# A vision tower on one core: GpSimd's sums of absolute differences, one image's set in two parts

## The reference, cut to what matters

```python
def one_query(qs):
    return -jnp.sum(jnp.abs(qs[:, None, :, :] - k), axis=-1) * scale
...
v = (x @ wqv_w.T + wqv_b).reshape(b, t, 3 * h, d)
q, vf, vb = (v[:, :, :h], v[:, :, h:2 * h], v[:, :, 2 * h:])
k = x[:, :, None, :] * wk[None, None]
a = _l1_scores(q, k)
a = jnp.concatenate([a, jnp.zeros((b, 1, t, h), a.dtype)], axis=1)
a = jax.nn.softmax(a, axis=1)[:, :t]
bf = jnp.einsum('bsdh,bshw->bdhw', a, vf)
bb = jnp.einsum('bdsh,bshw->bdhw', a, vb)
o = (bf + bb).sum(axis=2).reshape(b, t, d)
```

## Time and profile before

| | us |
|---|---|
| median of 3 runs | 2366.63 |
| lowest, highest | 2364.35, 2366.93 |
| the profiled execution, its whole time | 2366.79 |
| its span in the profile | 2365.0 |
| VectorE busy | 2054.4 (87%) |
| TensorE busy | 2158.9 (91%) |
| GpSimd busy | 1710.9 (72%) |
| ScalarE busy | 1693.7 (72%) |

### The profile page before, as it was taken

The page is one execution under the profiler, slowest core; times in us unless marked ns, Lnnn a source line. Parts: engine busy times, 40 slices in busy tenths (PEclk is TensorE's granted clock), DMA queues, the critical chain, the costliest instruction groups (busy, mean ns, idle before and its releaser), DMA issues.

```text
span 2365.0 us, 48508 instructions
## 1 busy us (share of the span) xinstructions
PE 2158.9 (91%) x13383; PEld 999.3 (42%) x13383; DVE 2054.4 (87%) x2501; ACT 1693.7 (72%) x4540; POOL 1710.9 (72%) x975
## 2 busy tenths in 40 slices
PE   5475999999888999999999999999999999999978
PEld 4352333333333444444444444444444444444456
DVE  2877777778879999999999999999999999999963
ACT  1232443333458888888888888888888888888865
POOL 0111433333468999999999999999999999999923
PEclk9797999999999999999999999999999999999979
DMA  4301333333312222222222222222222222222201
GB/s 130 84 1 36 77 78 77 77 75 73 73 48 52 52 53 57 57 53 54 53 56 57 55 54 53 55 57 56 53 53 54 57 57 54 53 53 57 57 12 30
DMA packets 169432, 135.54 MB, mean 57 GB/s; under 512 B 45661, under 2 KB 151070, under 8 KB 169247
## 3 DMA queue, kind: packets, MB, share of 16 engines
q1 hardware_dynamic: 159850, 118.02, 20.2%
q10 hardware_dynamic: 9532, 16.91, 3.0%
HBM read 10.51 MB, written 4.19 MB: 6 GB/s over the span
## 4 chain that ended last, share of the span: by engine, by line
DVE 32%; PE 31%; issue 11%; ACT 1%; DVEq 0%; SPq 0%; ACTq 0%; DMA 0%
DVE score L1673 30%; PE pp L943 9%; PE pp L931 4%; PE pp L880 3%; PE pp L849 3%; PE pp L842 2%; PE pp L875 2%; PE pp L1037 1%; PE pp L935 1%; PE pp L890 1%; PE pp L1028 1%; PE pp L734 1%; PE pp L1046 1%; PE pp L1020 0%; DVE absd L1621 0%
## 5 line engine op out<-in xcount | busy, mean ns | idle before, releaser
L1673 DVE TENSOR_REDUCE score<-pp 128x16 f32<-128x1024 f32 x1280 | 1480.0, 1214 | 80.8 <-PE pp L943 80.6
L1805 POOL TENSOR_TENSOR absd<-absd 128x2560 f32<-128x2560 f32 x635 | 1449.1, 2282 | 80.2 <-ACT absd L1252 39.4
L943 PE MATMUL pp<-blocks,pick 128*128 128x512 f16 x2560 | 757.3, 383 | 48.8 <-DVE score L1673 34.3
L1252 ACT ACTIVATE absd<-pp 128x512 f32<-128x512 f32 x1280 | 696.2, 599 | 78.3 <-PE pp L931 59.0
L931 PE MATMUL pp<-blocks,pick 128*128 128x512 f16 x1280 | 394.1, 381 | 1.8 <-ACT absd L1252 1.5
L943 PEld LDWEIGHTS pp<-blocks,pick 128*128 128x128 f16 x2560 | 192.1, 97 | 437.6 <-DVE score L1673 339.3
L1776 POOL TENSOR_TENSOR absd<-absd,yw 128x512 f32<-128x512 f32 x112 | 147.4, 1316 | 293.4 <-DVE yw L1605 293.2
L1196 ACT ACTIVATE absd<-pp 128x512 f32<-128x512 f32 x256 | 149.6, 597 | 205.0 <-PE pp L785 136.2
L1621 DVE SCALAR_TENSOR_TENSOR absd<-pp,absd 128x512 f32<-128x512 f32 x256 | 171.6, 686 | 76.0 <-ACT absd L1196 60.7
L931 PEld LDWEIGHTS pp<-blocks,pick 128*128 128x128 f16 x1280 | 119.0, 97 | 193.2 <-ACT absd L1252 43.3
L1282 ACT ACTIVATE expd<-attn 128x65 f32<-128x65 f32 x512 | 156.5, 315 | 0.0
(11 more groups left out here) (244 smaller groups left out, 2644.0 us busy)
## 6 DMA issues: line engine op xcount, KB each, us to landing
blocks<-qk SPq DMA_DIRECT2D x1032, 64.0 KB, 2.0
blocks<-gT SPq DMA_DIRECT2D x128, 128.0 KB
blocks<-gT ACTq DMA_DIRECT2D x128, 128.0 KB
attn<-score SPq DMA_DIRECT2D x256, 64.0 KB, 2.1
xs<-xn SPq DMA_DIRECT2D x66, 32.0 KB, 1.8
big<-in_wrb_t SPq DMA_DIRECT2D x1, 2064.0 KB
big<-in_x_rows SPq DMA_DIRECT2D x4, 512.0 KB, 6.0
token_rows<-big SPq DMA_DIRECT2D x8, 256.0 KB, 2.0
```

The lines of the kernel that those rows point to most:

```text
L943: mm = pe.matmul(ps[bank + n], pick[:, unit % 8 + n, :], blocks[:, b, unit // 16, unit // 8 % 2, :], start=True, stop=True)
L1252: nc.scalar.activation(absd[odd][:, 16 * u + 8 * n:16 * u + 8 * n + 8, :], ps[4 + n].rearrange("p (h w) -> p h w", w=D), ACT.Abs).then_inc ...
L1673: dve.tensor_reduce(score[:, odd, b, 16 * d:16 * d + 16], pp[:, bank:bank + 2, :].rearrange("p n (h w) -> p (n h) w", w=D), AX.X, ALU.add, ...
L1805: nc.gpsimd.tensor_tensor(x[:, :, 0:w], x[:, :, 0:w], x[:, :, w:2 * w], ALU.add).then_inc(X["tree"], 1)
```

## The change

Before, GpSimd waits for the absolute values of all five A tiles of an image, and sums the 80 rows with five additions and a sixth that writes to `score`. After, it takes the first three tiles (48 rows) when those are there, with five additions and a sixth, and then the other two (32 rows) when those are there, again with five and a sixth. The wait for the DMA that reads `score` stands before the first of the two writes, and "pooled" is counted once, by the second.

```diff
-                x = absd[b]
-                pool.wait_ge(X["abs"], 2 * NA * s + 2 * NP)
-                for m, w in enumerate((32, 16, 8, 4, 2)):
-                    if m:
-                        pool.wait_ge(X["tree"], 5 * s + m)
-                    nc.gpsimd.tensor_tensor(x[:, :, 0:w], x[:, :, 0:w], x[:, :, w:2 * w], ALU.add).then_inc(X["tree"], 1)
-                pool.wait_ge(X["tree"], 5 * s + 5)
-                if at >= 2:
-                    pool.wait_ge(X[f"spread{b}"], SPREAD * (p - 1))
-                nc.gpsimd.tensor_tensor(score[:, odd, b, 16 * ND:16 * ND + 16 * NP].unsqueeze(2), x[:, :, 0:1], x[:, :, 1:2],
-                                        ALU.add).then_inc(X["pooled"], 1)
+                x, n = absd[b], 10 * s
+                for lo, hi in ((0, 3), (3, NP)):
+                    part = x[:, 16 * lo:16 * hi, :]
+                    pool.wait_ge(X["abs"], 2 * NA * s + 2 * hi)
+                    for m, w in enumerate((32, 16, 8, 4, 2)):
+                        if m:
+                            pool.wait_ge(X["tree"], n + m)
+                        nc.gpsimd.tensor_tensor(part[:, :, 0:w], part[:, :, 0:w], part[:, :, w:2 * w], ALU.add).then_inc(X["tree"], 1)
+                    n += 5
+                    pool.wait_ge(X["tree"], n)
+                    if at >= 2 and lo == 0:
+                        pool.wait_ge(X[f"spread{b}"], SPREAD * (p - 1))
+                    op = nc.gpsimd.tensor_tensor(score[:, odd, b, 16 * (ND + lo):16 * (ND + hi)].unsqueeze(2), part[:, :, 0:1], part[:, :, 1:2],
+                                                 ALU.add)
+                op.then_inc(X["pooled"], 1)
```

## The result

The changed kernel takes 2526.55 us in the median of four runs (2525.83 to 2527.29), against 2366.32 (2364.35 to 2366.93) before: 1.0679 times as long, with a 95% interval of 1.066 to 1.0697. The profiled execution has a span of 2524.0 us. The prediction on record was 2520.

A forecast was written before the change was run, and what follows sets the result against it. VectorE with TensorE was taken as the bound, with GpSimd level and becoming the bound at B = 13.61 us a batch. Span 674.5 + 2.7 + 126 B + 125.7 = 2517.8, so 2520 us, 6.5% slower; range 2470 to 2565 us at 0.79.

The forecast's parts named there:

- The bound: Amid the stage VectorE with TensorE sets the period, 12.285 us an image; GpSimd needs 12.14 and has 0.14 to spare.
- The cost of a batch: GpSimd's additions for one image grow from 12.145 by 1.46 to 13.61 us, summed by instruction size.
- The upper end of the range: A batch of 13.97 us, from 0.30 us per added GpSimd instruction, giving 2565 us.
- What the price is: Each added GpSimd instruction costs about 0.25 us whatever its size, not a price per row.
- the rival of cheap instructions: Small GpSimd additions overlap, so a split costs little more than its gaps: 2392 to 2470 us, chance 0.11.
- The page's rule: Documentation's 4497 ns for a 2048-element GpSimd addition leaves 60 ns for the rest: batch 12.96, time 2438 us.
- Where the wait goes: In the stage ScalarE waits for GpSimd's buffers, about 1 us an image, TensorE behind it, VectorE behind TensorE; SyncE costs nothing.
- the 0.88 of the sum: TensorE's clock decides only under a mean of 12.0 / 13.61 = 0.88; that rival had chance 0.01.
- GpSimd never waits: Once behind, GpSimd finds an image's five tiles ready after 10.3 us, while its batch s starts 13.6 after.
- The tail: VectorE's last sum comes 14.1 us after batch 125, then 111.57 us unchanged to the end of the span.
- The rival on the other side: Hidden: buffers' 2.05 us and GpSimd's idle time in the head absorb its lag; time stays 2367 us, chance 0.03.
- the line through the whole stage: Span is 802.9 + 126 B, B being GpSimd's batch time; it reaches 2365.0 at B = 12.40.

The follow-up runs named there:

- The alternating order: Changed kernel's twelve additions and two waits, with the two parts' additions taken in turn, each waiting only for the last but one: 2392.97 us, ratio 1.0107.
- the four-and-one split: Changed kernel with its two parts cut as four tiles and one instead of three and two: 2528.18 us, ratio 1.069 to the kernel before.
- the changed kernel in the loop alone: Changed kernel with two parts only from image 7 on, images 0 to 6 summed whole as before: 2516.93 us, ratio 1.0636.
- one image in four: Changed kernel with two parts only for the second image of every odd pair, the others summed whole: 2400.86 us, ratio 1.0136.
- the seven additions: Kernel before with only the first addition split, into 1536 and 1024 elements, both after the wait for all five tiles: 2369.26 us, ratio 1.0008.
- the alternating loop: Alternating kernel with its order only from image 7 on, images 0 to 6 summed whole with six additions: 2366.88 us, ratio 0.9999 to the kernel before.
- the alternating ones: Twelve additions with the parts taken in turn, throughout (2392.97 us) or only in images 0 to 6 with the loop's sets whole (2390.68 us).

## Why the prediction was right

**The bound.** Right. GpSimd stood 0.14 us an image under the kernel's pace, and took the chain as soon as its batch grew. A kernel whose page has GpSimd at 72% had it at 12.14 of 12.285 us in the stage that counts.

**The cost of a batch.** Forecast 13.61, measured 13.62. By term, start to start: 1536 elements 3.541 forecast and 3.433 + 0.079 = 3.512 measured, 1024 2.461 and 2.429, 768 1.914 and 1.919, 512 1.363 and 1.350; the two writes 0.39 and 0.22 + 0.19 = 0.41. About 0.05 of the mean is a pause of 0.22 us at the turn of the loop, once in four batches, which the sum did not have at all; small errors the other way made up for it. The upper end of the range had a slip: 12.145 + 6 x 0.30 is 13.95, not 13.97.

**What the price is.** Half right. I called 0.25 us what an instruction costs whatever its size. The alternating order shows two parts. About 0.13 us is there only when an instruction needs the one just before: a gap of 0.079 and an overlap of 0.05 forgone. The rest, about 0.14 us, is the instruction's own: the twelve durations sum to 12.9 us, the six to 11.7, which is 0.19 each for six more, less 0.05 of overlap. The batch of six has five such steps, the one before the write with 0.14 instead of 0.08, 0.71 us together; the change adds six instructions and five such steps, 6 x 0.14 + 5 x 0.13 = 1.49 us, and the batch grew by 1.47. Alternation adds the six and takes the first five steps away, 0.84 - 0.71 = 0.13, and with the pause at the turn of the loop 0.18; the pace grew by 0.17 to 0.18, from 12.145 to 12.31 and 12.33. The 0.14 and 0.05 are worked out from means, and not measured one by one. The durations alone grew by 1.08 us, from 11.73 to 12.82, where the rival of cheap instructions had about 0.70. The forecast held because the change runs each part as a chain, like the rows that I read. The cheap rival had the right mechanism, overlap, for a program that was not this one.

**The page's rule.** The Trainium skill, "GPSIMD Engine Reference", section 3.1, has 4497 ns for an addition of 2048 elements. The trace of the four-and-one split has 4510: it agrees. But what I took from the page for the rest of an instruction, 60 ns, does not: 16 elements take 216 ns. The estimate from the page, 2438 us, was 89 us short.

**Where the wait goes.** Right along the whole line of waits, with ScalarE at 71.0 us in 600, or 1.6 us an image, where I had written about 1. TensorE's clock cost nothing, as forecast: it was 0.96 to 0.99 against the 0.88 of the sum. SyncE's queue cost nothing that shows: among the waits from 1200 to 1800 us none is for a DMA.

**GpSimd never waits.** Wrong in the head, right after it. Timeline of GpSimd, first parts of batches 0, 2, 4, 7 and 8:

```profile
672.88 7.52 POOL L1807 TENSOR_TENSOR absd<-absd 128x1536 f32<-128x1536 f32 x5 [12.49 <-ACT absd L1252]
...
700.85 8.37 POOL L1807 TENSOR_TENSOR absd<-absd 128x1536 f32<-128x1536 f32 x5 [1.05 <-ACT absd L1252]
...
731.83 7.46 POOL L1807 TENSOR_TENSOR absd<-absd 128x1536 f32<-128x1536 f32 x5 [2.29 <-ACT absd L1252]
...
776.13 9.20 POOL L1807 TENSOR_TENSOR absd<-absd 128x1536 f32<-128x1536 f32 x5 [2.67 <-ACT absd L1252]
...
791.42 7.51 POOL L1807 TENSOR_TENSOR absd<-absd 128x1536 f32<-128x1536 f32 x5
```

GpSimd waits 19.6 - 12.5 = 7.1 us for ScalarE in all, five times up to batch 7. Batch 8 starts at 791.42; the sum had 674.5 + 2.7 + 8 x 13.61 = 786.1, which is even earlier than the 787.33 of the kernel before. This is most of what the forecast lacked. Of the 6.2 us between spans of 2517.8 and 2524.0, the start was 1.6 us earlier, the eight batches 6.9 longer, the pace gave 1.2, and the tail took 0.3 back. One cause shows in VectorE's layer norm: L342, 0.17 us before, takes 2.56, L372 1.66 instead of 0.72, and L351 3.09 instead of 1.21. L351 begins while GpSimd's additions run:

```profile
716.62 3.09 DVE L351 TENSOR_TENSOR big<-xn 128x1024 f32<-128x1024 f32 x1
```

With L347 and L368, five instructions took 6.4 us more. I had costed only what these meetings take from GpSimd, not what they take from VectorE. With the head left whole, in the changed kernel in the loop alone, batch 8 started at 787.06, so the split head costs 4.4 us.

**The tail.** Batch 125 ends at 2398.36 + 0.24 = 2398.60, and VectorE's last sum begins 2412.21 - 2398.60 = 13.6 us later, forecast 14.1, and 111.8 to the end, forecast 111.57.

**The rival on the other side.** Its point was mis-sized. I put it at 12.40 us a batch, from the line through the whole stage; one image in four, at 12.566, gave 2400.86 where the line, with 1.8 us around the span, has 2388. With batch 10 at 811.90 and 116 batches behind it, as before, and 2 us of slack in the buffers, the point is 12.287 + 2 / 116 = 12.30, an estimate. It fits that the seven additions, at 12.29, kept the old pace, and that the alternating loop, at 12.31, had GpSimd as its bound. It changes nothing for the forecast, which was far above.

No version here beats the kernel before. The best, alternating in the loop, only equals it in time, and its stage is 5 us longer in the trace.

## What to carry to other kernels

An engine that is no bound by its share over the span may be level with the bound in the stage that counts; time one period of it there, start to start, before giving it more instructions. Starting a piece of work earlier is worth nothing on an engine that is behind anyway. If work has to be cut into more instructions on GpSimd, put pieces that do not need each other between those that do; but leave gaps where VectorE has such instructions as the layer norm's to run beside GpSimd.

## What the runs showed of the hardware

- A GpSimd instruction that needs the one just before starts 0.079 us after its end; one that does not starts about 0.05 us before the end of the other. Ahead of a write to `score` the gap was 0.08 or 0.16. Twelve additions took 13.62 us a batch as two chains and 12.33 alternating.
- VectorE's `tensor_scalar` and `tensor_tensor` on 16 elements in SBUF stood 10.2 to 11.4 us beside GpSimd additions without a gap, and ended within 0.5 us of the last of the ten, in two programs. With gaps of 0.079 us between the additions, in the changed kernel, the same two took 2.56 and 1.15 us; each ended within 0.05 us of the end of the addition that was running, at 689.78 and 763.35. The Trainium skill, "SBUF — State Buffer", section "SBUF: two separate sides", says of the shared pair of ports that the one who comes second blocks for the whole instruction of the other. The changed kernel agrees with that; in the alternating ones VectorE's instruction stood over many instructions of the other. That the gaps let VectorE in is what these programs show together; the ports themselves were not seen.
- The last stage, from VectorE's last sum to the end of the span, is the same code in every program and took 106.7 to 112.4 us. Between two of them 3 us went with a granted clock of 0.86 or 0.94 in the last stretch. So a difference of a few us between two programs' times can come from a stage that neither touches.
